# Order of the two score matmuls of a pair in a fused attention layer

## The reference

```python
# per sequence; x: [512, 256]
qkv = layernorm(x) @ qkv_w.T            # q, k, v: 16 heads, [512, 16] each
q, k = rotate(q), rotate(k)
attn = q @ k.T * 0.25 + min(key - query, 0) * slope[head] * 8
x = x + softmax(attn) @ v @ proj_w.T + proj_b
h = layernorm(x)
out = x + h @ W.T + b + (h @ V_r) @ C.T
```

## Time and profile before

| | us |
|---|---|
| median of 3 runs | 2108.87 (2107.6 to 2109.93) |
| span of the profiled execution | 2108.7 |
| PE busy | 2074.9 |
| DVE busy | 1855.8 |
| ACT busy | 1513.9 |
| POOL busy | 1296.4 |

### The profile page before, as it was taken

One profiled execution on the slowest core, in us unless ns is written; L12 is line 12 of the kernel. 1 busy time (PEld: TensorE's weight loads), 2 busy tenths in 40 slices (PEclk: granted clock), 3 DMA queues, 4 the chain that ended last, 5 costly groups with the idle time before them and its releaser, 6 DMA issues.

```text
span 2108.7 us, 81949 instructions
## 1 busy us (share of the span) xinstructions
PE 2074.9 (98%) x33596; PEld 1193.3 (57%) x33596; DVE 1855.8 (88%) x5459; ACT 1513.9 (72%) x2562; POOL 1296.4 (61%) x1093
## 2 busy tenths in 40 slices
PE   6999999999999999999999999999999999999998
PEld 3455555555555555555555555555555555555554
DVE  7899998988998998999898999998999999999972
ACT  2377777777777777787777777777777777777664
POOL 6357566667565667666666666666766666766512
PEclk8699999999999999999999999999999999999999
DMA  5343333433333433334333334334333334333311
GB/s 156 92 115 102 87 112 105 112 116 104 94 103 107 114 113 105 96 101 124 94 113 109 100 97 121 104 105 123 101 86 115 104 109 121 102 95 104 97 51 39
DMA packets 158935, 218.78 MB, mean 104 GB/s; under 512 B 19072, under 2 KB 104960, under 8 KB 158560
## 3 DMA queue, kind: packets, MB, share of 16 engines
q1 hardware_dynamic: 157280, 211.44, 35.5%
q10 hardware_dynamic: 1280, 2.10, 0.3%
HBM read 36.52 MB, written 16.78 MB: 25 GB/s over the span
## 4 chain that ended last, share of the span: by engine, by line
PE 91%; DVE 1%; ACT 1%; issue 1%; POOL 0%; DVEq 0%
PE ps_s L436 30%; PE ps_o L459 21%; PE ps_misc L413 18%; PE ps_misc L400 12%; PE ps_misc L387 3%; PE ps_misc L478 3%; PE ps_t L446 2%; PE ps_misc L469 2%; DVE junk L648 1%; ACT pt L840 0%; PE ps_t L519 0%; ACT x_res L788 0%; ACT x_res L783 0%; DVE x_hat L684 0%; DVE x_res L633 0%
## 5 line engine op out<-in xcount | busy, mean ns | idle before, releaser
L648 DVE CUSTOM_DVE_ANT_0 junk<-ps_s,alibi 128x512 bf16<-128x512 f32 x2004 | 1302.7, 687 | 185.7 <-PE ps_s L436 153.6
L840 ACT ACTIVATE pt<-ps_t 128x1024 f32<-128x1024 f32 x1024 | 1049.6, 1025 | 450.5 <-DVE ps_t L661 441.4
L446 PE MATMUL ps_t<-at 64*128 64x512 f32 x2048 | 762.2, 451 | 2.3 <-ACT pt L840 2.0
L436 PE MATMUL ps_s<-at 64*128 64x512 f32 x2004 | 757.7, 454 | 3.6 <-DVE row_max L648 2.8
L459 PE MATMUL ps_o<-pt,v_one 128*17 128x128 f32 x16384 | 637.4, 273 | 1.4 <-ACT pt L840 1.3
L459 PEld LDWEIGHTS ps_o<-pt,v_one 128*17 128x17 f32 x16384 | 441.1, 98 | 184.2 <-issue 46.0
L436 PEld LDWEIGHTS ps_s<-at 64*128 64x128 f32 x2004 | 325.6, 184 | 240.9 <-DVE row_max L648 133.4
L661 DVE TENSOR_TENSOR ps_t<-ps_t,diag 128x256 f32<-128x256 f32 x1024 | 435.5, 425 | 14.5 <-PE ps_t L446 14.4
L1006 POOL TENSOR_TENSOR rope_b<-raw,rope_sin 128x512 f32<-128x512 f32 x128 | 164.5, 1285 | 327.3 <-ACT raw L820 323.6
L1022 POOL TENSOR_TENSOR halves<-rope_a,swapped 128x512 fp32r<-128x512 f32 x126 | 159.3, 1287 | 322.8 <-DMA swapped<-rope_b 322.8
L446 PEld LDWEIGHTS ps_t<-at 64*128 64x128 f32 x2048 | 328.1, 184 | 13.9 <-ACT pt L840 8.7
(11 more groups left out here) (105 smaller groups left out, 1801.0 us busy)
## 6 DMA issues: line engine op xcount, KB each, us to landing
at<-halves SPq DMA_DIRECT2D x192, 512.0 KB, 4.0
swapped<-rope_b SPq DMA_DIRECT2D x256, 128.0 KB, 2.6
x_in<-in_L_attn_x_dram SPq DMA_DIRECT2D x32, 512.0 KB, 5.2
num<-o_sb SPq DMA_DIRECT2D x512, 32.0 KB
x_res<-in_L_attn_x_dram SPq DMA_DIRECT2D x32, 512.0 KB, 4.3
out_dram<-x_hat SPq DMA_DIRECT2D x32, 512.0 KB, 5.8
at<-spread_den SPq DMA_DIRECT2D x60, 64.0 KB
at<-max_t ACTq DMA_DIRECT2D x128, 16.0 KB
```

The costliest lines, as they stand in the source:

```text
L436: pe.matmul(scores_bank(n, t), operand(n, 0)[:, t * P:(t + 1) * P], operand(n, 1), start=True, stop=True).then_inc(s_done, 1)
L446: pe.matmul(ps_t[:, j, :], operand(n, 1)[:, j * P:(j + 1) * P], operand(n, 0), start=True, stop=True).then_inc(t_done, 1)
L648: dve.tensor_tensor_reduce(unused, scores_bank(n, t), alibi[:, off:off + N], 1.0, LOWEST, ALU.add, ALU.max, row_max[:, hb % 2, t, hh:hh + ...
L840: act.activation(pt[:, h % 2, 2 * pair:2 * pair + 2, :], ps_t[:, 2 * pair:2 * pair + 2, :], ACT.Exp).then_inc(exp_done, 1)
```

## The change

Inside the loop over the two tiles of a half, T is issued before S, where S was issued before T. The matmuls, their operands, semaphores and wait values stay as they are, and so does the text of all other engines.

```diff
                     for t in (2 * half, 2 * half + 1):
+                        if nt is not None:
+                            exp_scores(nt, t)
                         if n is not None:
                             max_scores(n, t)
-                        if nt is not None:
-                            exp_scores(nt, t)
```

## The result

| | before | after |
|---|---|---|
| median, us | 2107.81 (2104.95 to 2109.93, 5 runs) | 2119.19 (2115.81 to 2131.07, 5 runs) |
| ratio | | 1.0061, 95% interval 1.0037 to 1.0086 |
| forecast | | 2112.8 (2108.5 to 2117.5) |

The change costs time, as forecast, but the medians lie 11.4 us apart instead of 3.9, and the median is outside the range. The interval of the ratio allows 8 to 18 us.

The account below looks back on a forecast made before the run. PE, busy 98%, bounds most halves, with DVE close behind at 88%. Late T0 in the sequences, 1.7 us, plus the bare halves, 2.2, make 3.9 on 2108.9: forecast 2112.8 us, range 2108.5 to 2117.5.

Parts of the forecast that it names:

- the second effect: In each pair S comes second, its load up to 0.01 us later, returned at the half's end; taken as zero.
- Rival A: In all 1002 halves the offset inside a pair delays R unreturned: 4.0 us on top, 2116.8; chance 0.13.
- the prediction's loop: In bare halves, S0 waiting for T0 closes a two-half loop of 3.40 us instead of 3.11; together 2.2 us.
- boundary (at 1106.75): Sequence boundary where S0's delay passes through R, divide, D and E: T0 0.06 us later, 29 times, 1.7 us.
- place of the earlier trace: Place at 1117.05 with T0 0.10 us late; DVE is idle there and S1 has slack, so cost zero.
- The first effect: Where S1 waits and T1 doesn't, T1 streams meanwhile; at most 11.3 us gained, taken as zero.
- Rival B: Halves where S1 waits for R shrink by 0.10 us as T1 streams under the wait: 2101.5; chance 0.08.
- The third, the wait ahead of S0: Where T0 is late its wait now holds back S0 and R: 1.7 us in sequences, 2.2 in bare halves.
- C: Every late T0, in sequences and bare halves, is paid again in full: +19.2 us, 2128.1; chance 0.05.
- D: The loop through E has slack, so S0's delay is absorbed everywhere: 2108.9 us; chance 0.14.
- (a): Most frequent halves, with 16 or more extra matmuls, lasting 2.10 to 2.12 us; forecast unchanged at 2.10.
- (b): Paired halves with eight extra matmuls, S1 waiting for R in one: 1.77 + 1.67 = 3.44 us, forecast unchanged.

Follow-up runs that it names:

- e_waitfirst: Kernel before, order S0, T0, S1, T1 kept, with only the wait for E moved ahead of S0: 2117.03 us, ratio 1.0042.
- e_noinc: Changed kernel, order T0, S0, T1, S1, but T0 gives no semaphore signal and T1's stands for both: 2114.82 us, ratio 1.0030 to the kernel before.
- e_pair0: Kernel before with only the first pair of each half turned (T0, S0, S1, T1): 2129.33 us, ratio 1.0089.
- e_pair1: Kernel before with only the second pair of each half turned (S0, T0, T1, S1): 2109.56 us, ratio 1.0011.
- e_four: Kernel before with T first in only 4 of a sequence's 32 halves, each ahead of a half whose S1 waits: 2111.44 us, ratio 1.0015.
- b_fill: Kernel before with four additional matmuls, results unused, in T-only halves of the last sequence where PE waits for E: 2109.60 us, ratio 1.0002.

## Why the prediction was wrong

The step that failed is the second effect, "S is the second of its pair instead of the first", of which the prediction said "I take zero". Its mistake is twofold. It looked at the wrong distance: S's load is 0.01 us or less behind T's, but what R waits for is the semaphore, which is 34 ns behind. And it claimed that the late S is returned at the end of the half because S1 and not T1 is now ahead of the extra work. That fits the 2.10 us halves, which didn't change. But a loop that goes from S0's signal to R, R and the next half's S1 has no such return.

Rival A had the path, a later R that S1's end doesn't return, but not the cause: it took the delay to be that between the issues, some 4 ns, and not that of the signal, added 4 us (4 ns × 1002 halves), and said that it would decide itself in the 2.10 us halves. These didn't change; the delay shows in few places and is large there. That 2116.8 lies nearer to the result than the forecast is therefore in part luck. Per sequence, as means over 27 of them, the profile has:

| place | after | e_waitfirst | e_noinc | e_pair0 |
|---|---|---|---|---|
| 4 halves in which S1 waits | +0.124 | +0.008 | +0.012 | +0.134 |
| boundary (at 1106.75) | +0.078 | +0.057 | +0.063 | +0.077 |
| place of the earlier trace rows, 3 halves | +0.045 | +0.013 | +0.021 | +0.049 |
| 4 halves up to the first DEN half | +0.042 | -0.033 | +0.009 | +0.028 |
| whole sequence | +0.278 | +0.027 | +0.100 | +0.281 |

30 × 0.278 = 8.3 us; nearly all of the rest comes from the bare halves. In these the prediction's loop is 3.40 us, 3.41 with the wait alone and 3.44 in the changed kernel (2039.29 to 2042.73 below), again by the 34 ns, in the timeline of PEld of the kernel after:

```profile
2039.29 0.18 PEld L446 LDWEIGHTS ps_t<-at 64*128 64x128 f32 x1 [0.63 <-ACT pt L840]
...
2042.73 0.18 PEld L446 LDWEIGHTS ps_t<-at 64*128 64x128 f32 x1 [0.62 <-ACT pt L840]
```

A late T0 also takes the signals' delay on: at these places E, and through it D and R, is what PE waits for, so each should get about 0.03 longer. The second and third row differ by 0.02 and 0.03 between after and e_waitfirst, which fits. The fourth row differs by more, 0.075 or 2.3 us in all, and is not taken apart: there T0's lateness in the trace of before varies from sequence to sequence (up to 0.40 us), and e_pair1 and e_four, which don't wait ahead of S0 there, are also 0.031 and 0.034 below before.

Point by point:

- The first effect, nothing gained from T1 under S1's wait: right (e_pair1). Rival B is refuted.
- The second: wrong, some 6 to 9 us instead of 0. The body of after less that of e_waitfirst gives 8.6, the timed runs without a fall of the clock 6.5, and T0's signal alone 6.3 in the body (after less e_noinc).
- The third, the wait ahead of S0: right in mechanism, place and size. 3.9 forecast; in the body 3.2 measured against before and 4.5 against e_pair1, which has S0 first as well; the boundary 0.06 and 0.057; the loop 3.40 and 3.41. The place of the earlier trace rows costs 0.013 by e_waitfirst, where I had zero.
- C, every late T0 paid again, and D, nothing to be seen: neither happened.
- "Halves of kinds (a) and (b) unchanged": (a) right, (b) wrong; 1.81 + 1.67 instead of 1.77 + 1.67. The text named a pair that no longer adds up to 3.44 as what would make it wrong, and so it was.
- Bounds of 2110.9 to 2114.9 for the sum were too narrow since the second effect had no upper bound in them from the signal's side, though the records of semaphores were in the trace of before: T0's came 34 ns behind S0's there too.

A rule of the Trainium skill would have given the delay of the signal, though not its price. "TensorE: Matmul & The Clock Gate", Part 3, in the section on the cost of the per-tile semaphore tail, says that the increments of concurrent matmuls are written one after another, and fits 26.3 ns for each increment and 4.7 for each tile. By it, as an estimate, the second signal of a pair comes 31 ns behind the first, and 4.7 ns behind where the first would be if the first matmul gives none; the traces agree, with 34 and 7 ns. The prediction cited the 4 ns between starts from the same part (3 ns measured) and missed the section behind it.

What stays open: why the clock falls in some executions and not in others of one program, since the idle places ahead of it are the same in both (0.3 to 0.6 us each). How often it falls differs: 5 of 6 runs of e_pair0, 4 of 12 of e_pair1 and 4 of 11 of e_waitfirst, against 1 of 26 of before beside them; but 1 of 5 of the changed kernel, and 4 of 29 of before in the last group. Whether the order has a part in that wasn't tested. Open are also the 7 ns that stay in e_noinc, and the fourth row of the table.

## What to carry to other kernels

When two matmuls run side by side, issue the one first whose semaphore another engine is already waiting for: here the second's signal was late by 34 ns though it started only 3 ns later, and 25 of the waiter's 32 ns went when the first gave no signal. So a matmul whose completion nobody needs should give no signal ahead of one that matters. Price a reordering from the semaphore to the waiter's start, not from issue to issue, and then look for the few places where the waiter is late: four halves of 32 carried a quarter to a third of this loss. Before moving a waiting instruction ahead of another, close the loop that arises (here S, R, D, E, T) and compare its length to the pace that the stretch has now.

## What the runs showed of the hardware

- Two matmuls in opposite 64-row halves, issued 3 ns apart: semaphores at 511 and 545 ns, whichever of the two kinds was first. Without an increment on the first, the waiter of the second started 652 ns after the first matmul instead of 677.
- Four single f32 matmuls with all 128 rows and 512 columns cost 2.1 us together in b_fill, although each was put into 0.3 to 0.6 us of idle time: each held the T behind it back to 1.06 us after its own start.
- Four PE waits of 0.3 to 0.6 us within some 7 us were followed, in some executions, by 20.5 us at a granted clock of 0.5, and in others of the same length and place by none; where it fell, this made an execution longer by 8.8 us (76.6 against 67.8 us from half 1024 to the end).
- The same fixed gap of about 0.21 us in weight loading at the head of a half is put down to whichever engine the first instruction waits for: of the 133.4 us "for R" before it is 114 (541 gaps of about 0.21), of the 142.4 us "for E" after 110 (once in each of 522). That share isn't a wait for either engine.
